# Attention scores of a transformer layer: two heads side by side in halves of TensorE's rows, operands in two float32r parts

## The reference

```
q, k, v = x @ Wq.T, x @ Wk.T, x @ Wv.T            # 4 x 1024 x 32 heads x 16
q, k    = rope(q), rope(k)
scores  = q k^T / 4 + bias[h, i - j]              # bias where 0 <= i - j < 256; -inf where j > i
m       = max(max_j scores, off[h])
out     = sum_j exp(scores - m) v / (sum_j exp(scores - m) + exp(off - m))
x       = layernorm(x + out @ Wo.T)
x       = layernorm(x + quantised(x) @ quantised(Wff).T + bff)   # blocks of 32, 4-bit values
```

## Time and profile before

| what | value |
|---|---|
| median of three runs | 1916.54 us |
| the profiled execution: span of its instructions | 1914.6 us |
| TensorE matmul busy | 1736.2 us, 91% of the span |
| DVE busy | 1404.3 us, 73% |
| ACT busy | 878.6 us, 46% |
| chain that ended last: share of PE | 68% |
| chain: "issue" / DVE / POOL | 13% / 12% / 3% |
| mean granted TensorE clock | 0.946 of full speed |

### The profile page before, as it was taken

The page is one execution under the profiler, slowest core; times in us unless marked ns, Lnnn a source line. Parts: engine busy times, 40 slices in busy tenths (PEclk is TensorE's granted clock), DMA queues, the critical chain, the costliest instruction groups (busy, mean ns, idle before and its releaser), DMA issues.

```text
span 1914.6 us, 35268 instructions
## 1 busy us (share of the span) xinstructions
PE 1736.2 (91%) x9768; PEld 880.6 (46%) x9776; DVE 1404.3 (73%) x4121; ACT 878.6 (46%) x1148; POOL 256.0 (13%) x122
## 2 busy tenths in 40 slices
PE   7999999489989998998998998999899999787762
PEld 3444444125545554554554554555455554343331
DVE  2444444698878887887887887888788771679996
ACT  2333333115545554554554554555455556344442
POOL 4333233300000000000000000000000000034442
PEclk9999999669999999999998999999999999899996
DMA  5445345714332522442334323252253201111111
GB/s 196 160 140 169 132 169 150 193 31 80 62 60 46 110 46 47 93 76 47 76 63 77 70 54 64 49 103 46 47 105 64 46 24 45 61 55 66 66 66 44
DMA packets 124695, 157.81 MB, mean 82 GB/s; under 512 B 14928, under 2 KB 80528, under 8 KB 124240
## 3 DMA queue, kind: packets, MB, share of 16 engines
q1 hardware_dynamic: 124496, 155.45, 34.3%
HBM read 104.15 MB, written 50.46 MB: 81 GB/s over the span
## 4 chain that ended last, share of the span: by engine, by line
PE 68%; issue 13%; DVE 12%; POOL 3%; ACT 1%; DMA 1%; DVEq 1%; SPq 0%; POOLq 0%; ACTq 0%
PE ps L643 14%; PE ps L680 14%; PE ps L658 13%; PE ps L619 12%; PE ps L663 12%; DVE junk L1118 2%; DVE mx L1111 2%; PE ps L768 2%; POOL probs L987 1%; PE ps L690 1%; DVE ps L1131 1%; POOL probs L1028 1%; DMA attn<-wvT 1%; DVE stats L1303 1%; POOL k_stack L1032 1%
## 5 line engine op out<-in xcount | busy, mean ns | idle before, releaser
L856 ACT ACTIVATE probs<-ps 128x1024 f32<-128x1024 f32 (+3 forms) x768 | 615.8, 813 | 562.4 <-PE ps L663 309.3
L1118 DVE CUSTOM_DVE_ANT_0 junk<-ps,bias_q 128x384 bf16<-128x384 f32 (+2 forms) x1024 | 503.7, 502 | 137.3 <-PE ps L643 124.1
L663 PE MATMUL ps<-bias_r,ident_r 128*128 (+3 forms) x1920 | 539.9, 368 | 0.0
L643 PE MATMUL ps<-k_stack,q_stack 96*128 96x384 bf16 (+3 forms) x1536 | 504.8, 347 | 35.0 <-DVE mx L1118 17.1
L658 PE MATMUL ps<-q_stack,k_stack 99*128 99x512 bf16 (+3 forms) x1536 | 496.8, 333 | 22.3 <-issue 19.8
L1111 DVE TENSOR_REDUCE mx<-ps 128x1 f32<-128x128 f32 (+3 forms) x768 | 365.0, 485 | 40.9 <-PE ps L643 32.5
L663 PEld LDWEIGHTS ps<-bias_r,ident_r 128*128 128x128 f32 x1920 | 338.0, 195 | 64.2 <-issue 1.7
L619 PE MATMUL ps<-attn 128*128 128x512 f32 x768 | 332.6, 596 | 10.7 <-DMA attn<-hT 9.8
L680 PE MATMUL ps<-probs,v_sb 128*32 128x512 f32 (+3 forms) x3072 | 327.3, 498 | 4.4 <-ACT probs L856 4.4
L643 PEld LDWEIGHTS ps<-k_stack,q_stack 96*128 96x128 bf16 x1536 | 143.4, 98 | 393.6 <-DVE mx L1118 197.7
L619 PEld LDWEIGHTS ps<-attn 128*128 128x128 f32 x768 | 146.7, 191 | 195.8 <-issue 195.8
(11 more groups left out here) (88 smaller groups left out, 1050.2 us busy)
## 6 DMA issues: line engine op xcount, KB each, us to landing
q_stack<-q_parts SPq DMA_DIRECT2D x192, 128.0 KB, 4.1
v_dram<-v_sb SPq DMA_DIRECT2D x32, 512.0 KB, 2.7
v_sb<-v_dram SPq DMA_DIRECT2D x32, 512.0 KB, 9.1
q_parts<-q_stack SPq DMA_DIRECT2D x96, 128.0 KB, 1.9
k_parts<-k_stack SPq DMA_DIRECT2D x96, 128.0 KB, 2.0
k_stack<-k_parts SPq DMA_DIRECT2D x32, 384.0 KB, 7.1
attn<-hT SPq DMA_DIRECT2D x8, 1024.0 KB, 6.0
k_stack<-k_parts SPq DMA_DIRECT2D x32, 256.0 KB, 7.8
```

The source lines that it names most:

```text
L643: pe.matmul(ps_ring[:, use.bank, 0:c1 - c0], q_stack[0:STACK, b, hl, I * P:(I + 1) * P], k_stack[0:STACK, b, hl, c0:c1], start=True, stop= ...
L663: mm = pe.matmul(ps_s[:, u % 2, hh, 0:bw], ident_r[:, :], rhs, start=False, stop=(s == 1))
L856: act.activation(probs[:, (u // 2) % 3, 2 * pr:2 * pr + 2, 0:w], ps_s[:, pr, :, 0:w], ACT.Exp).then_inc(exp_done, 1)
L1118: ins = dve.tensor_tensor_reduce(out=junk[:, use.bank, 0:c1 - lo], in0=ps_ring[:, use.bank, lo - c0:c1 - c0], in1=bias_q[:, hl, BAND - t0 ...
```

## The change

- **Two float32r parts.** `PARTS` is 2, in DRAM and in the stacks, with 4 bytes each. The contraction has 3 x 16 = 48 rows (query parts 0,0,1 against key parts 0,1,0), or 50 with the shift's two parts. In phase 1 the second ACT copy and one DVE subtraction per pair are gone (`low_part` takes the place of `rest` and `third_part`).
- **Two heads side by side.** Of a group's four heads, `place(hl)` puts heads 0 and 1 at partitions 0 to 63 and heads 2 and 3 at 64 to 127. The two products of a unit in `scores` and each pair of `maxima` stand one behind the other, the one in rows 0 to 63 of the array and the other in rows 64 to 127. In the built program they have the tile size 64 x 128 at positions 0 and 64. Before, every one had 128 x 128.
- **All bias on TensorE.** `biases` adds it for both heads of a unit, four products of 128 x 128 in a row. `add_bias`, `bias_k` and the semaphores `last_head_scored` and `biased` are gone.
- **Order of the stream.** A unit is: two scores, then a pair of maxima (two pairs in units 10 and 21, none in 22 and 23), then the four bias products, then as before `pv` and the transposes.
- The stacks have the same size in bytes; `load_stack` is ten DMAs instead of nine, `load_shift` four instead of three, phase 1 stores four instead of six per pair, of twice the bytes each. Small buffers are laid over others to make room.

```diff
-PARTS = 3
-STACK = 6 * D
+PARTS = 2
+STACK = 3 * D
 ROWS = STACK + PARTS
+HALF_ROWS = P // 2
-Q_PART = (0, 0, 0, 1, 1, 2)
-K_DMAS = ((0, 3), (3, 2), (5, 1))
+Q_PART = (0, 0, 1)
+K_DMAS = ((0, 2), (2, 1))
...
 def units_beside(u):
-    ks = list(range(min(NM, NM * u // SPREAD), min(NM, NM * (u + 1) // SPREAD)))
-    return ks[:1], ks[1:]
+    pairs = NM // 2
+    return [k for j in range(min(pairs, pairs * u // SPREAD), min(pairs, pairs * (u + 1) // SPREAD))
+            for k in (2 * j, 2 * j + 1)]
...
-                    I, c0, c1 = MAX_UNITS[k % NMU]
-                    hl = k // NMU
+                    hl, I, c0, c1 = max_unit_of(k)
+                    x, p = place(hl)
+                    rows = slice(HALF_ROWS * x, HALF_ROWS * x + STACK)
...
-                    pe.matmul(ps_ring[:, use.bank, 0:c1 - c0], q_stack[0:STACK, b, hl, I * P:(I + 1) * P],
-                              k_stack[0:STACK, b, hl, c0:c1], start=True, stop=True).then_inc(ring_filled, 1)
-
-            def scores(g, b, n, u, between):
+                    pe.matmul(ps_ring[:, use.bank, 0:c1 - c0], q_stack[rows, b, p, I * P:(I + 1) * P],
+                              k_stack[rows, b, p, c0:c1], start=True, stop=True).then_inc(ring_filled, 1)
+
+            def scores(g, b, n, u):
...
-                for hh in ((1, 0) if u % 2 else (0, 1)):
-                    hl = 2 * (u % 2) + hh
-                    on_pe = bw and hl < HG - 1
-                    mm = pe.matmul(ps_s[:, u % 2, hh, 0:w], k_stack[0:ROWS, b, hl, J * P:(J + 1) * P],
-                                   q_stack[0:ROWS, b, hl, i0:i0 + w], start=True, stop=not on_pe)
-                    if on_pe:
-                        for s in range(2):
-                            rhs = bias_r[:, bass.ds(g % 2, 1), s, hl, b0:b0 + bw].rearrange("p a c -> p (a c)")
-                            mm = pe.matmul(ps_s[:, u % 2, hh, 0:bw], ident_r[:, :], rhs,
-                                           start=False, stop=(s == 1))
-                    if hl == HG - 1:
-                        mm.then_inc(last_head_scored, 1)
-                    if hh == u % 2:
-                        between()
-                mm.then_inc(scored, 1)
+                for x in range(2):
+                    rows = slice(HALF_ROWS * x, HALF_ROWS * x + ROWS)
+                    mm = pe.matmul(ps_s[:, p, x, 0:w], k_stack[rows, b, p, J * P:(J + 1) * P],
+                                   q_stack[rows, b, p, i0:i0 + w], start=True, stop=not bw)
+                if not bw:
+                    mm.then_inc(scored, 1)
+
+            def biases(g, u):
...
+                for x in range(2):
+                    for s in range(2):
+                        rhs = bias_r[:, bass.ds(g % 2, 1), s, head_in(x, p), b0:b0 + bw]\
+                            .rearrange("p a c -> p (a c)")
+                        mm = pe.matmul(ps_s[:, p, x, 0:bw], ident_r[:, :], rhs, start=False, stop=(s == 1))
                 mm.then_inc(scored, 1)
...
-                        inner, behind = units_beside(u) if more else ((), ())
-                        scores(g, b, n, u, lambda: maxima(ga, ba, inner, use_of))
+                        scores(g, b, n, u)
+                        if more:
+                            maxima(ga, ba, units_beside(u), use_of)
+                        biases(g, u)
...
-                        maxima(ga, ba, behind, use_of)
...
-            def add_bias(g, n, T):
-
-                b0, bw = band_cols(T)
-                if T == 0:
-                    dve.wait_ge(bias_split, 3 * (g + 1))
-                dve.wait_ge(last_head_scored, n * NT + T + 1)
-                tile = ps_s[:, 1, 1:2, 0:bw]
-                dve.tensor_tensor(tile, tile, bias_k[:, bass.ds(g % 2, 1), b0:b0 + bw],
-                                  ALU.add).then_inc(biased, 1)
```

206 lines of the change are left out of this document (105 added, 101 removed).

## The result

| | before | changed |
|---|---|---|
| median of the runs | 1916.62 us | 2245.84 us (2237.12 to 2255.42) |
| ratio | | 1.172, 95% interval 1.1685 to 1.1756 |
| profiled execution, span | 1914.6 us | 2248.1 us |
| mean granted TensorE clock | 0.946 | 0.869 |
| phase 2 | 417.7 to 1631 us | 417.2 to 1963.7 us |

The forecast was 2024 us with 1822 to 2085 as its range. The direction was right, the size was not: the time lies 161 us beyond the range. Phase 2 begins 0.5 us earlier, and phase 3 takes 283.6 and 284.4 us, so all of it came in phase 2. In the table of the experiments the time is the median of all executions of a kernel and the ratio goes by its fast ones alone (of e9 two of four, 2065 and 2094 us), so the two can differ.

The account below looks back on a forecast made before the run. PE's product stream was taken to bound phase 2. Thirty rounds at +3.3 us (+99), the last two rounds (+11) and phase 1 (-3) gave +107 on 1914.6, about 2024 us with the 1.9 us around it; range 1822 to 2085.

Parts of the forecast that it names:

- Halves side by side: Scores and maxima on PE: a pair streams in one product's time, -3.8 and -3.9 us per round.
- not side by side: Rival for scores and maxima: the two halves run one behind the other, nothing saved there; 2215 us, chance 0.11.
- Fourth head's bias: Bias products on PE: adding the fourth head's bias there costs +2.9 us per round.
- Mode changes, 32 x 0.17 and v's blocks: PE's tile mode: 32 more changes per round, +5.4 us, and loads after twelve probabilities-times-v blocks, +1.0; together +6.4.
- the rival of 1928: Rival for PE's mode changes: drain of 0.105 us each, float32r loads hidden in it; about 1928 us, chance 0.14.
- Phase 1: Its tail has one ACT copy and one DVE subtraction less: -3 us once, bounds -8 to +5.
- Ring: PE waiting for DVE to read maxima, mainly units 8 to 11: 2.6 us for 0.9, +1.7 per round, bounds +0.5 to +3.
- Nothing for the clock: TensorE clock: no term for a changed clock; phase 3 and the loop's turn put at nothing.
- my +3.3: Sum of all terms for one round of phase 2: +3.3 us, applied to thirty rounds as +99.

Follow-up runs that it names:

- e9: Changed kernel with exactly one pair of maxima in each of the 24 units, the shift's transposes two units later; 2095.2 us.
- e1: Kernel before with only the fourth head's bias moved to TensorE and DVE's `add_bias` gone (wrong values); 1989.6 us.
- e5: Changed kernel with the maxima's pairs placed by a table: none in four units, two in units 3, 15, 17 and 19, one elsewhere; 2173.1 us.
- e3: Changed kernel with DVE reading only 64 columns of each maximum (wrong row maxima); 2014.2 us.
- e16: Changed kernel with DVE reading only 64 columns for the 12 maxima of units 8 to 11 (wrong row maxima); 2056.8 us.
- e15: e10 with the score pairs of units 9 and 11 computed 2 and 3 more times, same values; 1980.5 us.
- e10: Changed kernel with one pair of maxima in each unit and the bias products in 64-row halves too; 2024.5 us.
- e13: Changed kernel with the score pairs of units 9, 10 and 11 computed 2, 3 and 4 more times, same values; 2142.0 us.
- e14: e9 with the score pairs of units 9 and 11 computed 2 and 3 more times, same values; 2059.6 us.
- e17: e13 with unit 21's score pair also computed 3 more times; 2142.2 us.
- e8: e5 with TensorE's loop written over two groups and no other edit; 2191.1 us.
- e4: Kernel before with maxima products over 64 of their 96 rows, one at a time in 64-row mode (maxima incomplete); 2208.3 us.

## Why the prediction was wrong

By its own steps, per round, in the order in which it gave them:

- **Halves side by side, -7.7**: right. Starts 2 to 4 ns apart, 0.24 from pair to pair. The rival "not side by side" is out, though the measured time was nearest to its 2215: a time that agrees with a rival does not show the rival.
- **Fourth head's bias, +2.9**: right (+2.45 in e1 with what DVE gives back).
- **Mode changes, 32 x 0.17 and v's blocks, +6.4**: right in kind, 13% small. 0.195 each gives 32 x 0.025 = 0.8 more. A float32r load of 195 ns does not hide, so the rival of 1928 is out, and 0.105 for the load is the part that I had estimated as 0.065.
- **Phase 1, -3 once**: it was 0.5, inside the bounds.
- **Ring, +1.7 (2.6 in place of 0.9)**: too small, and read in the wrong way. By the starts of one round PE waits about 3.6 us: 0.8 in unit 9, 1.5 in units 10 and 11 (forecast 2.2 for units 8 to 11, so nearly right), 1.0 in unit 21 (forecast 0.4), the rest in small pieces. That is +2.7, inside the bounds of 0.5 to 3. I had followed DVE's backlog; what counts is that two pairs in a row wait for one whole read, with or without a backlog. e5 and e9 show it.
- **Nothing for the clock**: this is the step that failed. The prediction prices each instruction at full clock and puts phase 3 and the loop's turn at nothing. It never asked what short waits of PE do to the clock of the stream behind them, though rows 1 have the column and it counted a cold clock into the turn. The runs showed 431 us of phase 2 at half clock in place of 55, worth about 150 to 158 us.

The sum closes within some 10 us. Warm rounds: measured 42.3 - 36.85 = +5.45 for my +3.3, and 30 x 2.15 = 64 us. (Stream alone: 42.3 - 3.6 = 38.7 against 36.85 - 0.9 = 35.95, +2.7 for my +1.6, of which 0.8 is the mode changes; the last 0.3 was not followed.) Clock: (431 - 55) x 0.42 = 158 us. Together 222, and 2024 + 222 = 2246. By the stretches of 42.65 it is 30 x 2.5 = 75 us for the rounds and some 148 us, 0.39 for 1 us at half clock, for the clock, again about 2247. The profiled execution took 2249.9. So the clock is two thirds of the miss. The other third is ring and mode changes, and even without the clock it would have brought the time to about 2088, just beyond the range's end of 2085.

That the half clock comes from PE's idle stretches in the ring is shown from three sides: shorter reads take both away (e3), shorter reads in units 8 to 11 alone do (e16), and useless work in the place of the idle time takes the half clock away without shortening a round (e15 against e10, clear in every execution; e13 takes it away behind units 8 to 11 of the changed kernel itself; e14 and e17 agree by their profiles). The last one also rules out DVE's reads as such, since they all stay. The Trainium skill has this in TensorE: Matmul & The Clock Gate, "A second HAM failure mode: psum-queue depth-cycling": cycling through PSUM banks leaves TensorE briefly idle between groups, often enough that its clock oscillates. The trace agrees with it: ahead of the fall stand three waits with starts 0.67 to 0.71 us apart, in e9 two of 0.7 us, in e5's last group and in e8 two for ACT with score starts 0.70 and 0.91 us apart. Behind the four doubled pairs of e5, 0.8 to 0.97 us each and several us apart, it did not fall. The same waits do not always bring it down (e9 in 8 of 21 rounds, e8 in 3 of 21 and e5 in none of them with the same instructions), so it isn't a matter of the instructions alone, and what decides in such a case stayed open.

Of the kernels with halves that leave nothing out, none beats the one before. The best, e15, is 3.4% slower, with one mode for everything but v, one pair per unit and filled waits.

## What to carry to other kernels

A wait on the engine that sets the pace has two prices, its length and the clock behind it: here 2.7 us more of waiting per round brought 377 us more at half clock, about 150 us, nearly half of the 329 us that the change cost. When a change adds short waits close together on TensorE, give the clock a term or a rival of its own, and test it by filling the wait with a repeated product. When products are made in pairs, a ring of three banks is one pair and a half: two pairs in a row then wait for a full read, so spread the pairs evenly one by one, and count the float32r load beside the drain (0.105 and 0.09 us here) for each change of tile mode.

## What the runs showed that was not expected

- A change between 64-row halves and the whole array costs 0.09 us, and a float32r load behind it 0.105 more; the records of the bias' loads are 189 to 195 ns long.
- Bias in two halves of the rows, crossed, streams at the time of the whole-array form: two pairs of 384 columns at 0.17 to 0.18 each in place of two products.
- 1 us at half clock costs about 0.4 us (0.42 by the rounds, 0.39 by the sum), not 0.5. That part of a round, as the waits for DVE, does not scale with it is the likely reason and was not measured by itself.
- Behind the turn of the loop the clock was at half for 3 to 17 us in most kernels and for 38 to 41 us in e4. That stays open.
